# Moving the gate weights of a mixture-of-experts stage from the product to u2's operand, two experts per operation

## What is computed

```python
probs = softmax(x @ gate_w + gate_b)                 # 16 experts
top_probs, top_idx = top_k(probs, 2)
top_probs = top_probs / sum(top_probs)
dispatch = sum(one_hot(top_idx, 16) * top_probs[..., None], axis=-2)
h1 = einsum('bsd,edh->bseh', x, w1)                  # 64 -> 128, for every expert
h2 = einsum('bsd,edh->bseh', x, w2)
hidden = silu(h1) * h2
expert_out = einsum('bseh,eho->bseo', hidden, w3)    # 128 -> 64
return einsum('bseo,bse->bso', expert_out, dispatch)
```

## Time and profile before

| | |
|---|---|
| median of 3 runs | 104.0 us (103.03 to 105.31) |
| the profiled execution | 104.42 us |
| its span in the trace | 102.7 us |
| mean granted TensorE clock | 0.983 of 2.4 GHz |
| busy: TensorE / VectorE / ScalarE / GpSimd | 92.6 / 71.0 / 52.8 / 45.3 us |
| first up starts | 47.74 us |
| last matmul ends | 100.24 us |

### The profile page before, as it was taken

One profiled execution on the slowest core, in us unless ns is written; L12 is line 12 of the kernel. 1 busy time (PEld: TensorE's weight loads), 2 busy tenths in 40 slices (PEclk: granted clock), 3 DMA queues, 4 the chain that ended last, 5 costly groups with the idle time before them and its releaser, 6 DMA issues.

```text
span 102.7 us, 2617 instructions
## 1 busy us (share of the span) xinstructions
PE 92.6 (90%) x954; PEld 50.9 (50%) x954; DVE 71.0 (69%) x218; ACT 52.8 (51%) x110; POOL 45.3 (44%) x57
## 2 busy tenths in 40 slices
PE   5977796999999999999992999979999999999990
PEld 4567685767758557765220353223333233333590
DVE  1347999797844929935899937999666877574451
ACT  0564978735366690657763145971445744451400
POOL 5868002211200410000459690871949699959100
PEclk9999999999999999999999589999999999999999
DMA  1569994000000000000799940000199990001002
GB/s 26 87 108 207 187 171 73 0 0 0 6 0 0 6 3 0 6 0 13 182 421 437 402 195 3 3 0 6 65 316 426 437 402 10 0 0 51 6 0 51
DMA packets 9514, 11.07 MB, mean 108 GB/s; under 512 B 6014, under 2 KB 8206, under 8 KB 8734
## 3 DMA queue, kind: packets, MB, share of 16 engines
q1 hardware_dynamic: 8492, 10.66, 33.8%
q10 hardware_dynamic: 914, 0.20, 0.9%
q0 software_dynamic: 96, 0.04, 0.8%
HBM read 10.57 MB, written 0.33 MB: 106 GB/s over the span
## 4 chain that ended last, share of the span: by engine, by line
PE 70%; DVE 12%; ACT 4%; DMA 3%; issue 3%; SPq 2%; POOL 2%; POOLq 0%; DVEq 0%
PE bank L953 27%; PE bank L972 11%; PE bank L910 4%; PE bank L853 4%; PE bank L883 3%; DMA wv_in<-in_L_conv_wv 3%; PE bank L746 3%; PE bank L838 3%; DVE qk L586 2%; PE bank L738 2%; PE bank L867 2%; DVE nmax L600 2%; PE bank L927 2%; PE bank L994 2%; PE bank L1004 2%
## 5 line engine op out<-in xcount | busy, mean ns | idle before, releaser
L406 POOL TENSOR_TENSOR hid<-uu,dbc 128x512 f32<-128x512 f32 x24 | 32.3, 1376 | 12.7 <-DVE uu L677 6.0
L953 PE MATMUL bank<-s2T,w_in 64*64 64x512 f32 x256 | 31.9, 617 | 0.8 <-ACT sil L502 0.7
L502 ACT ACTIVATE sil<-bank 128x512 f32<-128x512 f32 x32 | 19.0, 597 | 17.2 <-PE bank L953 15.0
L677 DVE TENSOR_TENSOR uu<-bank,sil 128x512 f32<-128x512 f32 x32 | 21.7, 688 | 8.9 <-ACT sil L502 5.6
L397 POOL TENSOR_TENSOR rstd<-veps,neg_half 128x2 f32<-128x2 f32 x8 | 5.6, 697 | 34.8 <-DVE veps L533 34.8
L953 PEld LDWEIGHTS bank<-s2T,w_in 64*64 64x64 f32 x256 | 9.3, 137 | 18.5 <-issue 12.1
L972 PE MATMUL bank<-hid,w_in 64*64 64x512 f32 x120 | 15.0, 591 | 0.0
L972 PEld LDWEIGHTS bank<-hid,w_in 64*64 64x64 f32 x120 | 4.6, 133 | 7.7 <-issue 6.7
L626 DVE TENSOR_TENSOR omega<-bank,tri 128x256 f32<-128x256 f32 x16 | 5.7, 416 | 1.6 <-PE bank L853 1.6
L688 DVE TENSOR_TENSOR hid<-uu,dbc 128x512 f32<-128x512 f32 (+1 forms) x9 | 6.5, 732 | 0.0
L473 ACT ACTIVATE qs<-bank 128x512 f32<-128x512 f32 x8 | 4.3, 594 | 2.9 <-PE bank L838 2.8
(11 more groups left out here) (125 smaller groups left out, 133.5 us busy)
## 6 DMA issues: line engine op xcount, KB each, us to landing
dbc<-dispatch_scratch SPq DMA_DIRECT2D x6, 1024.0 KB, 8.8
dbc<-dispatch_scratch SPq DMA_DIRECT2D x4, 512.0 KB, 4.5
w_in<-in_L_ffn_w SPq DMA_DIRECT2D x3, 512.0 KB, 8.1
x_in<-in_x ACTq DMA_DIRECT2D x1, 192.0 KB, 2.6
q_in<-in_L_attn_Q SPq DMA_DIRECT2D x2, 64.0 KB, 3.6
e_in<-in_L_attn_E SPq DMA_DIRECT2D x1, 128.0 KB, 4.3
out<-x SPq DMA_DIRECT2D x1, 128.0 KB, 2.0
out<-x SPq DMA_DIRECT2D x2, 64.0 KB, 1.7
```

Of the source, the lines that this page charges most:

```text
L406: nc.gpsimd.tensor_tensor(hid[:, i % HID], uu[:, i % UU], dbc[:, e, :], ALU.mult).then_inc(hid_done, 1)
L502: nc.scalar.activation(sil[:, i % SIL], banks[U1_BANK[i % 2]][:], ACT.Silu).then_inc(sil_done, 1)
L677: nc.vector.tensor_tensor(uu[:, i % UU], banks[U2_BANK[i % 3]][:], sil[:, i % SIL], ALU.mult).then_inc(uu_done, 1)
L953: last = nc.tensor.matmul(banks[bank[i % len(bank)]][C * c:C * (c + 1), :], w_in[rows, HIDDEN * e + C * c:HIDDEN * e + C * (c + 1)], s2T[r ...
```

## The change

- From unit 8 on, the gate weight is no longer put on the product, but on u2's operand: w2 (x * weight) instead of (w2 x) * weight. GpSimd multiplies `s2T` by the weight (step **scale**, into `scaled`, four buffers), and the matmul of u2 reads `scaled`. The matmul of u1 still reads `s2T`.
- One scale serves two units. Units are put in pairs, unit 2k with expert k and unit 2k+1 with expert k+8 (`expert_of`). `w_in` holds for experts 0 to 7 w1 in rows 0 to 63 and w2 below, and for experts 8 to 15 the other way round. So u2 of the even unit reads the lower 64 partitions of `scaled`, and that of the odd unit the upper 64, and one 128x512 operation weighs both.
- From unit 8 on, times writes `hid` itself (in two pieces for the last unit), and there is no weigh. Units 0 to 7 keep it, seven of them on GpSimd and unit 3 on VectorE.
- The up of a unit from 8 on waits for the scale of its pair.
- The weights are spread in two forms: for units 0 to 7 four loads of 512 KB on 128 partitions into `dbc` (now with 2 KB in a piece, as the two experts of a pair don't stand side by side), for pairs 4 to 15 loads into `pair_dbc`, each on 64 partitions: 512 KB twice for pairs 4 to 7, 256 KB twice for 8 and 9, 256 KB twice for 10 and 11, 512 KB twice for 12 to 15. Together 3 MB in the first half and 2 MB in the second, and those of the second wait for no buffer.
- `SCHEDULE` and `BANKS` are written anew for the whole program, and three idle matmuls after "project qk" 0 are now six after "transpose x" 3. The four loads of w1 and w2 are 256 KB each instead of two of 512 KB.

What does not change in number: matmuls of every kind but the idle ones (three more), silu, times, steps of the first two layers.

```diff
-CHUNKS = (0, 2, 4, 8, 12, 16)
+WEIGHED = 8
+WEIGHED_CHUNKS = (0, 2, 4, 8)
+PAIR_CHUNKS = ((4, 8), (8, 10), (10, 12), (12, 16))
+def expert_of(unit):
+    at = unit % EXPERTS
+    return at // 2 + EXPERTS // 2 * (at % 2)
 def on_dve(unit):
-    return unit % 4 == 3
+    return unit >= WEIGHED or unit in (3,)
...
-     ("residual 2", 3), ("up", 1), ("silu", 1), ("times", 0), ("up", 2), ("silu", 2), ("times", 1), ("up", 3),
+     ("residual 2", 2), ("untranspose sum", 3), ("residual 2", 3), ("up", 0), ("load silu", 0), ("up", 1),
...
+        def wait_scale(eng, pair):
+            half = pair // 8
+            eng.wait_ge(pair_ld[pair_chunk(pair)], 32)
+            if pair % 8 == 0 or pair == WEIGHED // 2:
+                wait_emptied(eng, "s2T", 2 * half)
+                wait_emptied(eng, "s2T", 2 * half + 1)
+            if pair - SCALED >= WEIGHED // 2:
+                eng.wait_ge(u2_filled, 2 * (pair - SCALED) + 2)
...
+                    if i == 0:
+                        for c in range(len(WEIGHED_CHUNKS) - 1):
+                            first, last = WEIGHED_CHUNKS[c] // 2, WEIGHED_CHUNKS[c + 1] // 2
+                            for k in range(last - first):
+                                src = d_scratch[0, first + k::EXPERTS // 2, :].unsqueeze(0).to_broadcast([P, 2, HALF])
+                                sp.dma_start(dbc[:, 2 * (first + k):2 * (first + k + 1), :], src).then_inc(dbc_ld[c], 16)
+                    for c, (start, stop) in enumerate(PAIR_CHUNKS):
+                        if start // 8 == i:
+                            pairs = slice(start % 8, start % 8 + stop - start)
+                            for r in range(2):
+                                src = d_scratch[i, EXPERTS // 2 * r + pairs.start:EXPERTS // 2 * r + pairs.stop, :]
+                                sp.dma_start(pair_dbc[C * (1 - r):C * (2 - r), start:stop, :].rearrange("p e t -> p (e t)"),
...
+                if name == "scale" and not scaled_on_dve(i):
+                    wait_scale(pool, i)
+                    nc.gpsimd.tensor_tensor(scaled[:, i % SCALED], s2T[:, HALF * (i // 8):HALF * (i // 8 + 1)], pair_dbc[:, i, :],
+                                            ALU.mult).then_inc(scaled_by_pool, 1)
...
+                if name == "times" and i >= WEIGHED:
+                    dve.wait_ge(u2_filled, i + 1)
+                    dve.wait_ge(sil_done, i + 1)
                     if i >= HID:
                         dve.wait_ge(down_done, (i - HID) // 2 + 1)
                     pieces = (slice(0, HALF),) if i < UNITS - 1 else (slice(0, HALF // 2), slice(HALF // 2, HALF))
                     for cols in pieces:
-                        nc.vector.tensor_tensor(hid[:, i % HID, cols], uu[:, i % UU, cols], dbc[:, e, cols],
-                                                ALU.mult).then_inc(hid_by_dve, 1)
+                        last = nc.vector.tensor_tensor(hid[:, i % HID, cols], banks[U2_BANK[i % 3]][:, cols], sil[:, i % SIL, cols],
+                                                       ALU.mult)
...
+                    if i >= WEIGHED:
+                        wait_scaled(pe, i // 2)
                     for m, bank, full in ((0, U1_BANK, u1_filled), (1, U2_BANK, u2_filled)):
-                        rows = slice(C * m, C * (m + 1))
+                        r = (m + i) % 2
+                        rows = slice(C * r, C * (r + 1))
+                        if m == 1 and i >= WEIGHED:
+                            moving = scaled[rows, i // 2 % SCALED, :]
+                        else:
+                            moving = s2T[rows, half * HALF:(half + 1) * HALF]
```

More of the change, by code:

```diff
@@ L40, with full_chunk, pair_chunk @@
 QUARTERS = TILES * CHUNKS_OF_TILE
-SIL, UU, HID = 3, 8, 8
-CHUNKS = (0, 2, 4, 8, 12, 16)
-def chunk_of(expert):
-    return sum(expert >= start for start in CHUNKS[1:])
+SIL, UU, HID, SCALED = 3, 8, 8, 4
+WEIGHED = 8
[4 more added lines that the diff above has]
+    return at // 2 + EXPERTS // 2 * (at % 2)
+def full_chunk(unit):
+    return sum(unit >= start for start in WEIGHED_CHUNKS[1:])
+def pair_chunk(pair):
+    return [pair < stop for start, stop in PAIR_CHUNKS].index(True)
@@ L287, in wait_hid, with wait_scaled @@
         def wait_hid(eng, unit, piece=0):
-            before = sum(on_dve(n) for n in range(unit + 1))
+            if unit >= WEIGHED:
+                eng.wait_ge(uu_done, unit + 1 + piece)
+                return
+            by_dve = sum(on_dve(n) for n in range(unit + 1))
             if on_dve(unit):
-                eng.wait_ge(hid_by_dve, before + piece)
+                eng.wait_ge(hid_by_dve, by_dve)
             else:
-                eng.wait_ge(hid_done, unit + 1 - before)
+                eng.wait_ge(hid_done, unit + 1 - by_dve)
+        def wait_scale(eng, pair):
[6 more added lines that the diff above has]
+                eng.wait_ge(u2_filled, 2 * (pair - SCALED) + 2)
+        def wait_scaled(eng, pair):
+            by_dve = sum(scaled_on_dve(n) for n in range(WEIGHED // 2, pair + 1))
+            if scaled_on_dve(pair):
+                eng.wait_ge(scaled_by_dve, by_dve)
+            else:
+                eng.wait_ge(scaled_by_pool, pair + 1 - WEIGHED // 2 - by_dve)
         def img(b):
@@ L315, in _ @@
             sp.dma_start(e_in[:], E.rearrange("h i k -> i h k")).then_inc(ld_e, 16)
[L316 to L318 removed]
+            for m in range(2):
+                for k, w in enumerate((w1, w2) if m == 0 else (w2, w1)):
+                    experts = slice(EXPERTS // 2 * m, EXPERTS // 2 * (m + 1))
+                    sp.dma_start(w_in[C * k:C * (k + 1), experts, :], w[experts].rearrange("e c h -> c e h")).then_inc(ld_w, 16)
             sp.dma_start(gate_in[:], gate_w).then_inc(ld_gate, 16)
@@ L671, in _ @@
                                             ALU.mult).then_inc(disp_ready, 1)
-                if name == "times":
+                if name == "times" and i < WEIGHED:
                     dve.wait_ge(u2_filled, i + 1)
@@ L678, in _ @@
                                             ALU.mult).then_inc(uu_done, 1)
-                if name == "weigh" and on_dve(i):
-                    half, e = divmod(i, EXPERTS)
-                    dve.wait_ge(uu_done, i + 1)
-                    dve.wait_ge(dbc_ld[half][chunk_of(e)], 16)
+                if name == "times" and i >= WEIGHED:
+                    dve.wait_ge(u2_filled, i + 1)
+                    dve.wait_ge(sil_done, i + 1)
                     if i >= HID:
@@ L971, in _ @@
                         for n in range(2):
-                            last = nc.tensor.matmul(banks[Y_BANK[r]][C * n:C * (n + 1), :], w3_in[rows, e + n, :],
+                            last = nc.tensor.matmul(banks[Y_BANK[r]][C * n:C * (n + 1), :], w3_in[rows, expert_of(2 * i + n), :],
                                                     hid[rows, (2 * i + n) % HID], start=(e == 0), stop=(e == last_pair))
```

141 lines of the change are left out of this document (75 added, 66 removed), and 14 rows, old and new, of tables (BANKS, SCHEDULE).

## The result

The changed kernel takes 113.76 us (median of 4 runs, 112.43 to 116.27), the kernel before 104.66 beside it (4 runs, 103.03 to 105.65): a ratio of 1.088, with a 95% interval of 1.065 to 1.112. The forecast was 102.1 with a range to 104.4, so both the number and the sign are wrong.

A forecast was written before the change was run, and what follows sets the result against it. TensorE was taken as the bound, with 5.7 us lost in the expert layer: 0.3 from the front plus 5.7 less about 4.1 lost anew gave 1.9 us less, 102.1 against the median of 104.0; range 99.6 to 104.4.

The forecast's parts named there:

- The start of the layer: Expert layer's first units: up 0 at 47.4, 0.3 us earlier; layer norm in 1.2 to 2 us, TensorE's 3 us wait gone.
- What is late next: Before up 8: `dbc` loads there at 55.0, pair loads take 4.2 us, weights there at 60.2, up 8 from 61.6.
- the bound of 61.8: Late end for the pair weights' arrival, with their loads at 182 GB/s; 60.2 was forecast.
- The clock: TensorE idle before up 8: if its clock falls, ups lose 1.4 us, the end is 1.1 later, 103.2; even chances.
- GpSimd's pace and the rest: From scale 4: six GpSimd operations, 8.0 us, up 14 at 68.2; then 30.1 us of TensorE work without interruption.
- The sum: Whole kernel: last matmul at 68.2 + 30.1 = 98.3 instead of 100.24, 1.9 us less.
- Rival 1: Pair loads run at the full 425 GB/s, weights there at 58.5: 3.6 us less, 100.4; chance 0.34.
- Rival 2: Swapped rows cost TensorE quadrant overlap between ups, up to 0.21 us at each of about 31 changes: 108; chance 0.06.
- Rival 3: First half's pair loads at 182 GB/s and the clock falls: weights at 61.8, time 104.8; chance 0.11.

The follow-up runs named there:

- a_dbc_contig: The changed kernel with each `dbc` load taking two neighbouring experts instead of two 16 KB apart (wrong experts for most of units 0 to 7); 109.24 us.
- a_serial: The changed kernel with the first half's pair loads issued only when all `dbc` loads have landed; 112.80 us.
- fix8_split: The changed kernel with units 0 to 7 on experts 0 to 3 and 8 to 11, and the first pair loads cut in two; 105.70 us.
- b_halves: The kernel before the change, each `dbc` load split into two of 64 partitions; 108.19 us.

## Why the prediction was wrong

**The start of the layer: right.** Up 0 came at 47.05 (forecast 47.4: the front gained 0.7 and not 0.3), the layer norm's four operations took 1.11 us, and TensorE didn't wait for them.

**"What is late next": the right wait, the wrong size.** It was said that up 8 would wait for scale 4, and scale 4 for the pair loads. It does. But scale 4 starts at 68.60 and not 60.2, later than the bound of 61.8. Two terms of this step failed. The first is the `dbc` loads: "The four loads for units 0 to 7 are 2.10 MB: the other 1.40 take 3.3 us, to 55.3" took the earlier trace rows's 425 GB/s for loads whose source is laid out differently. The change says `first + k::EXPERTS // 2`, a stride of eight rows, and the step gave it no price and no bound. By a_dbc_contig it is 7.7 us. The second is the 64 partitions: I took 252 GB/s for them (4.2 us), which isn't far from the 209 to 254 measured, but counted it for the pair loads alone. a_serial shows the `dbc` loads ahead of them, with rows 16 KB apart, landing 6 us later. With the Trainium skill's rule of half the ports ("SBUF — State Buffer", section on the DMA port swizzle) the forecast had 60.9, and that would have misled as well, as it too was applied to the 1.05 MB only.

That 252 was near is in part luck. It was read as the rate of w1 and w2, but these two loads were in flight together, one on each half of the partitions, and the row with 182 also holds the load of w3, on 128 partitions. The queue of the kernel before:

```profile
6.07 1.35 SPq L317 DMA_DIRECT2D w_in<-in_L_ffn_w  x2
...
9.35 0.59 SPq L320 DMA_DIRECT2D w_in<-in_L_ffn_w  x1
```

**The clock.** "If it falls, the ups behind lose 1.4" was left out of the number, as even chances. The wait became 8.23 us, not 3.3, and the clock fell: the two ups at 70.00 took 3.47 instead of 1.72, 1.75 lost, and none of it covered by GpSimd's pace. The 3.3 forecast would have been near the border: behind a wait of 2.81 us at this place the clock stayed at 1.00 (fix8_split), behind one of 4.43 it was 0.50 (a_dbc_contig, 65 to 67 us).

**GpSimd's pace and the rest: right.** The six operations from scale 4 on took 7.4 us (forecast 8.0), but TensorE, at half clock, was the slower one and reached up 14 only at 78.3, 9.7 after scale 4. From there to the last matmul it is 30.3 us, forecast 30.1. The sum again with what was measured: 98.3, plus 8.4 for the weights, plus 1.7 for the way to up 14, plus 0.2, is 108.6; measured 108.58.

**The rivals.** Rival 1 (full rate for the pair loads) is refuted by the 254 GB/s of a_serial, where they go alone, and by b_halves' 209 to 238. Rival 2 (the swapped rows) too: two ups at full clock still take 1.72 us, in the changed kernel as before. Rival 3 was right in kind, late weights and a fallen clock, and had 0.11; its worst rate, 182, was put on the pair loads alone. It ended at 104.8 since nothing in it touched the loads ahead.
